# Values as the stationary operand in two attentions, and one block of instructions for the layers and what follows

## The reference

```
x = x + L0_xattn(layernorm(x))   # 4 layers, each: rmsnorm, causal self attention (16 heads of 8), bias
                                 #   rmsnorm, cross attention over the context rows a window allows
                                 #   rmsnorm, silu(gate) * up, down;   after the layers a last rmsnorm
x = x + L0_attn(layernorm(x))    # ternary attention: u, v factors, sigmoid of products, sums
x = x + L0_ffn(layernorm(x))
x = x + L1_xattn(context, layernorm(x))   # 2 heads of 64, 1601 context rows a batch
x = x + L1_attn(layernorm(x))    # causal self attention, 16 heads of 8
x = x + L1_ffn(layernorm(x))     # 8 experts of 512, the best two are summed

def sdpa(q, k, v, bias):
    s = einsum('bhqd,bhkd->bhqk', q, k) * scale + bias
    p = softmax(s)
    return einsum('bhqk,bhkd->bhqd', p, v)
```

## Time and profile before

| | us |
|---|---|
| median of 3 runs | 509.67 (509.57 to 510.04) |
| profiled execution, its own time | 507.16 |
| profiled execution, span | 505.0 |
| TensorE (PE) busy | 463.1, 92% |
| VectorE (DVE) busy | 360.1, 71% |
| ScalarE (ACT) busy | 267.4, 53% |
| GpSimd (POOL) busy | 227.3, 45% |

### The profile page before, as it was taken

How to read it: one execution, slowest core, us unless ns; L and a number is a source line. 1 busy time by engine, 2 the same in 40 slices (tenths; PEclk the granted TensorE clock), 3 DMA queues, 4 the chain that set the end, 5 groups by cost and what they waited for, 6 DMA issues and landing times. The chain is left out here.

```text
span 505.0 us, 14335 instructions
## 1 busy us (share of the span) xinstructions
PE 463.1 (92%) x5430; PEld 400.6 (79%) x5430; DVE 360.1 (71%) x1028; ACT 267.4 (53%) x714; POOL 227.3 (45%) x342
## 2 busy tenths in 40 slices
PE   0899999999999999939899898999999999899997
PEld 0777896788778876929898787888888988689997
DVE  4286668566856685547788778998899987584644
ACT  3367756775777577613334455655555564432221
POOL 1393149315821682133599431749889511220000
PEclk9899999999999999969999999999999999999999
DMA  7800120102019000012202431040220000000000
GB/s 221 298 3 2 38 70 17 32 11 83 3 42 388 11 3 2 1 51 94 69 3 70 137 126 65 2 132 1 67 68 1 2 2 1 1 2 1 12 0 12
DMA packets 10031, 27.07 MB, mean 54 GB/s; under 512 B 1425, under 2 KB 4838, under 8 KB 9702
## 3 DMA queue, kind: packets, MB, share of 16 engines
q1 hardware_dynamic: 9958, 26.09, 15.4%
HBM read 25.82 MB, written 0.26 MB: 52 GB/s over the span
## 5 line engine op out<-in xcount | busy, mean ns | idle before, releaser
L893 POOL TENSOR_TENSOR rstd<-ss,par 128x1 f32<-128x1 f32 x52 | 28.6, 551 | 103.0 <-ACT sq L729 103.0
L749 ACT ACTIVATE pr<-sd 128x512 f32<-128x512 f32 x56 | 34.6, 627 | 6.0 <-DVE sd L802 5.6
L1264 POOL TENSOR_TENSOR xh<-xh,rsx 128x512 f32<-128x512 f32 (+1 forms) x32 | 29.8, 930 | 4.6
L1781 POOL TENSOR_TENSOR rstd<-mv,par 128x1 f32<-128x1 f32 x21 | 5.3, 250 | 57.6 <-DVE mv L1616 48.0
L1260 POOL TENSOR_TENSOR xh<-cx,mvx 128x512 f32<-128x512 f32 (+1 forms) x32 | 30.8, 962 | 0.7
L733 ACT ACTIVATE h<-y,rstd 128x128 f32<-128x128 f32 x48 | 19.2, 400 | 9.8 <-POOL rstd L893 9.3
L1239 DVE BATCH_NORM_STATS2 stx<-cx 128x6 f32<-128x128 f32 x104 | 22.7, 275 | 0.7 <-DMA cx<-ctx_in 0.7
L887 POOL TENSOR_TENSOR kblk<-qk,cf 128x512 f32<-128x512 f32 x20 | 20.9, 1043 | 0.9
L879 POOL TENSOR_TENSOR qk<-rope 128x256 f32<-128x256 f32 x20 | 14.5, 726 | 13.7 <-DVE rope L786 13.6
L1249 POOL TENSOR_TENSOR rsx<-rsx,par 128x13 f32<-128x13 f32 x8 | 20.1, 2516 | 0.6
L729 ACT ACTIVATE sq<-y 128x129 f32<-128x129 f32 x52 | 15.9, 307 | 8.4 <-DVE y L833 6.7
(11 more groups left out here) (566 smaller groups left out, 1522.8 us busy)
## 6 DMA issues: line engine op xcount, KB each, us to landing
cx<-ctx_in SPq DMA_DIRECT2D x13, 768.0 KB
we<-we_in SPq DMA_DIRECT2D x8, 514.0 KB, 8.7
wc<-wc_in SPq DMA_DIRECT2D x4, 768.5 KB, 5.9
wa<-wa_in SPq DMA_DIRECT2D x5, 387.0 KB, 3.0
wb<-wb_in SPq DMA_DIRECT2D x4, 256.5 KB, 4.1
uvT<-uvT_in SPq DMA_DIRECT2D x1, 1024.0 KB, 4.8
uv<-uv_in SPq DMA_DIRECT2D x1, 1024.0 KB, 6.8
cx<-ctx_in SPq DMA_DIRECT2D x13, 32.5 KB
```

Of the source, the lines that this page charges most:

```text
L749: nc.scalar.activation(pr[:, t, at:at + 512], sd[:, t, at:at + 512], ACT.Exp).then_inc(s[piece], 1)
L893: nc.gpsimd.tensor_tensor(rstd[:, t:t + 1], ss[:, t:t + 1], par[:, 1:2], ALU.pow).then_inc(s[piece], 1)
L1264: nc.gpsimd.tensor_tensor(part, part, rsx[:, b, tiles].unsqueeze(2).to_broadcast(shape), ALU.mult).then_inc(xm["c_normed"], 1)
```

## The change

1. `weigha`, `weighb` and `cweigh` swap their operands: the values (32 columns) are stationary, the turned weights stream (64 columns), each result lands in 32 rows of PSUM, already turned. The sums come from four more matmuls for each of the three pieces, with a constant block of ones `ones8` stationary and 128 columns streaming.
2. `recip` and `crecip` take the reciprocal of 128 x 128 in place of 128 x 16; `o` and `co` write `oT` directly. `turn_o` and `oT` are gone; `cturn_o` and `coT` are left to `whole` alone.
3. The values' bias is added in `vblk` (layers) and no longer in `oT`; it is loaded with `bo`, in two DMAs where there was one. The rows of `Wo` are reordered on the host to fit.
4. The first block: one zeroing activation (2048 columns) for two (1152 each), no memsets of ones, one more load for `ones8`.
5. The second and third block are one. `opening` runs the layers, then each engine goes on with what follows, with no barrier between. The queues are joined: `JOIN` = 3547581.86 is added to the places of what follows, so on each engine all pieces of the layers stand ahead of all that follow. Banks are handed out over the joint queue. `z_moments`, `z_power` and `z_norm` of tile 3 now stand with those of the others.
6. All tables of places are new, of the layers and of what follows. `th` has two buffers, and `qh` is made in place; the context is reloaded behind `c_normed` where it was behind `c_center`.

Core of the diff:

```diff
-PERIOD, SKEW = 94.96, (0.0, 6.64, 13.36, 19.85)
+PERIOD, SKEW = 95.07, (0.0, 6.64, 13.28, 19.91)
...
-FINAL = {"PE": {}, "ACT": {"square_f": 233.37}, "DVE": {"norm_f": 235.66, "x_f": 248.65, "z_moments": 253.29, "z_norm": 346.43},
-         "POOL": {"pow_f": 468.90, "z_power": 528.02}}
+FINAL = {"PE": {}, "ACT": {"square_f": 2709.04}, "DVE": {"norm_f": 16.76, "x_f": 18.75, "z_moments": 23.76, "z_norm": 32.91},
+         "POOL": {"pow_f": 678.03, "z_power": 5874.90}}
...
+JOIN = 3547581.86
+class Joint:
+    def __init__(self):
+        self.queue = {e: sorted([(w, 0, l, t, p) for w, l, t, p in FAST.queue[e]] + [(JOIN + w, 1, i, g, p) for w, i, g, p in LAST.queue[e]])
+                      for e in AT}
+        self.first = {e: 1 + max(n for n, z in enumerate(q) if z[1] == 0) for e, q in self.queue.items()}
...
-        q2 = sb("q2", [P, T, 2, P])
-        vblk = sb("vblk", [P, T, 2, 8, 2, 9])
+        vblk = sb("vblk", [P, T, 2, 8 * 32])
+        ones8 = sb("ones8", [P, 80])
+        q2 = sd[:, :, 0:2 * P].rearrange("p t (g q) -> p t g q", g=2)
...
-                for j in range(4 * (half == "b"), 4 * (half == "b") + 4):
-                    for b in range(2):
-                        last = nc.tensor.matmul(bank[L * b:L * b + L, 18 * j:18 * j + 18], pts[:, t, P * j + L * b:P * j + L * b + L],
-                                                vblk[:, t, b, j, :, :], start=True, stop=True)
+                for b in range(2):
+                    for k in range(4):
+                        j = 4 * half + k
+                        at = 32 * j - 16 * half
+                        nc.tensor.matmul(bank[32 * k:32 * k + 32, L * b:L * b + L], vblk[:, t, b, at:at + 32],
+                                         pts[:, t, P * j + L * b:P * j + L * b + L], start=not half and b == 0, stop=True, skip_group_check=True)
+                for k in range(4):
+                    j = 4 * half + k
+                    last = nc.tensor.matmul(bank[32 * k:32 * k + 32, P:2 * P], ones8[:, 16 - 16 * half:48 - 16 * half], pts[:, t, P * j:P * j + P],
+                                            start=False, stop=True, skip_group_check=True)
...
-                        last = nc.tensor.matmul(bank[L * b:L * b + L, 36 * g:36 * g + 36], pts[:, t, P * g + L * b:P * g + L * b + L],
-                                                vcblk[:, 2 * t + b, g, :, :], start=True, stop=True)
+                        nc.tensor.matmul(bank[32 * g:32 * g + 32, L * b:L * b + L], vcblk[:, 2 * t + b, g, :],
+                                         pts[:, t, P * g + L * b:P * g + L * b + L], start=b == 0, stop=True, skip_group_check=True)
+                for g in range(4):
+                    last = nc.tensor.matmul(bank[32 * g:32 * g + 32, P:2 * P], ones8[:, 48:80], pts[:, t, P * g:P * g + P],
+                                            start=False, stop=True, skip_group_check=True)
...
             elif piece in ("recip", "crecip"):
-                nc.vector.reciprocal(rv[:, t, :], ops[:, :, 8]).then_inc(s[piece], 1)
+                nc.vector.reciprocal(qk[:, t, 0, :], held(od, k, l, t)[:, P:2 * P]).then_inc(s[piece], 1)
             elif piece in ("o", "co"):
-                nc.vector.tensor_tensor(o[:, t, :].rearrange("p (h d) -> p h d", d=HD), ops[:, :, 0:8],
-                                        rv[:, t, :].unsqueeze(2).to_broadcast([P, H, HD]), ALU.mult).then_inc(s[piece], 1)
+                nc.vector.tensor_tensor(oT[:, t, :], held(od, k, l, t)[:, 0:P], qk[:, t, 0, :], ALU.mult).then_inc(s[piece], 1)
...
-            elif piece == "oT":
-                act.wait_ge(s["turn_o"], n)
-                nc.scalar.activation(oT[:, t, :], held(od, "turn_o", l, t)[:, 0:P], ACT.Identity,
-                                     bias=A[:, A_BV:A_BV + 1]).then_inc(s["oT"], 1)
...
-            dve.wait_ge(s["zeroed"], 2)
-            for a in range(2):
-                nc.vector.memset(vblk[64 * a:64 * a + 64, :, :, :, a, 8:9], 1.0)
-            for a in range(4):
-                nc.vector.memset(vcblk[32 * a:32 * a + 32, :, :, a, 8:9], 1.0)
...
         with nc.Block() as block:
             @block.tensor
             def _(pe):
+                def whole():
...
+                either(pe, lambda: opening(pe, x_pe_piece, pe_piece, "PE"), whole)
                 x_queue(pe, x_pe_piece, pe_piece, "PE")
```

More of the change, by code:

```diff
@@ L108, in __init__ @@
     def __init__(self, engines, when):
-        self.queue = {e: sorted((when(p, l, t), l, t, p) for p, layers in pieces for l in layers for t in range(T)
-                                if p[:2] != "z_" or t < T - 1)
+        self.queue = {e: sorted((when(p, l, t), l, t, p) for p, layers in pieces for l in layers for t in range(T))
                       for e, pieces in engines.items()}
@@ L142 @@
 XAHEAD = 3
[L143 to L149, removed]
-YAT = {
[L151 to L181, removed]
@@ L564, in take @@
                 return x_take(pe, piece, t, 0)
-            for p, i, j in od.bank[piece, l, t][2]:
-                pe.wait_ge(s[p], one(i, j))
+            for kind, p, i, j in od.bank[piece, l, t][2]:
+                if kind:
+                    x_wait(pe, p, x_count(p, i, j))
+                else:
+                    pe.wait_ge(s[p], one(i, j))
             return held(od, piece, l, t)
@@ L1478, in x_act_piece @@
             elif piece == "un0":
+                if i < 2:
+                    act.wait_ge(s["y3" if i else "y2"], one(LAYERS - 1, T - 1))
                 x_wait(act, "v1", i - 1)
@@ L1834, in _, with whole @@
             def _(act):
+                def whole():
+                    general(act, act_piece, "ACT", act_any)
+                    ahead(act, x_act_piece, "ACT")
+                either(act, lambda: opening(act, x_act_piece, act_piece, "ACT"), whole)
                 x_queue(act, x_act_piece, act_piece, "ACT")
@@ L1838, in _, with whole @@
             def _(dve):
+                def whole():
+                    general(dve, dve_piece, "DVE", dve_any)
+                    ahead(dve, x_dve_piece, "DVE")
+                either(dve, lambda: opening(dve, x_dve_piece, dve_piece, "DVE"), whole)
                 x_queue(dve, x_dve_piece, dve_piece, "DVE")
@@ L1842, in _, with fast, whole @@
             def _(pool):
+                pool_bias(pool, 0)
+                def fast():
+                    zero_context(pool)
+                    opening(pool, x_pool_piece, pool_piece, "POOL")
+                def whole():
+                    pool_queue(pool, GENERAL)
+                    pool.wait_ge(s["y3"], one(LAYERS - 1, T - 1))
+                    zero_context(pool)
+                    ahead(pool, x_pool_piece, "POOL")
+                either(pool, fast, whole)
                 x_pool_start(pool)
```

321 lines of the change are left out of this document (197 added, 124 removed).

## The result

The changed kernel takes 502.16 us (median of four runs, 501.93 to 503.84) where the kernel before takes 509.83: ratio 0.9885, 95% interval 0.9859 to 0.9910. (That ratio and its interval are the record's; the two medians by themselves give 0.9850.) Predicted were 501.1 us and faster. In two later groups of runs the ratio was 0.9916 (0.9888 to 0.9944) and 0.9887 (0.9856 to 0.9919).

A forecast was written before the change was run, and what follows sets the result against it. TensorE was taken to bound the layers. Start -0.9, layers -2.8, boundary -4.5 and last part -0.4 sum to -8.6: 507.16 becomes 498.56, plus 2.51 gives 501.1 us; own range 497 to 505, for all 494.5 to 512.

The forecast's parts named there:

- offset of 2.51: Added to the sum because the profiled execution took 507.16 us and the median of the runs shown was 509.67.
- Start: First block: without DVE's memsets, TensorE's first matmul comes earlier, -0.9 us.
- TensorE in the layers: TensorE's queue: -1.4 us a layer, 0.98 from dropping turn_o and 0.4 from shorter weigh and cweigh, four strips at once.
- The reciprocal's duration: DVE in each attention: 128 columns take 0.97 us, +0.7; bounds 0.29 and 2.0.
- What of it is exposed: Layers: one of eight reciprocals a layer on the path, in self attention where DVE is near full, +0.7 us a layer.
- The new order: New places of everything else: 0, with 4 us allowed either way; as a rival, losing had chance 0.10, 505 to 510.
- The boundary: Between layers and what follows: barrier and waiting go, DVE's branch remains; along 4.5 us earlier, bounds 3.1 and 7.
- The last part: Four self attentions behind the layers: -0.5 for turn_o, -0.2 for eight halves, +0.3 for reciprocals, together -0.4 us.
- DVE taking over: Rival, chance 0.12: reciprocals exposed in the attentions, between shift and the next tile's max; slower from 17 exposed, 513 with 21.
- No low clock: Rival, chance 0.20: reciprocals covered and TensorE keeps the full clock level after its shorter pause; -14.2, 495.5 us.
- Two strips: Rival, chance 0.08: weigh and cweigh run two strips at once instead of four, 0.45 us more each, +25, 527 us.
- The first rival: Reciprocals covered and no low clock behind the layers, chance 0.20: -14.2, 495.5 us.

The follow-up runs named there:

- second profile: The changed kernel, unchanged, profiled once more; span 499.1 us, against 502.0 in its first profile.
- old places and copies: Changed kernel with its layers queued by the earlier kernel's places, and a plain copy replacing each attention reciprocal: 495.25 us, ratio 0.9786.
- order strip by strip: Changed kernel with the value matmuls of weigh and cweigh ordered so both key halves follow directly in one strip: 505.22 us.
- old places: Changed kernel with only its layers queued by the earlier kernel's places, period and skew: 499.9 us, ratio 0.9850; again 498.24 us, 0.9826.

## Why the prediction came out as it did

The sign was right and the total lies in the range, but its closeness is in part luck. The sum said -8.6. By medians the gain was 7.7 us in the first group of runs and 4.1 and 6.2 in the two later ones; by the ratios it was 4.3 to 5.9; by the spans it is 3.0 with the late dip and 5.9 in the second profile. Against that second profile the layers came out 6.3 us worse than forecast (+3.5 for -2.8), the boundary 1.1 better (counted to `M1`) and the rest 2.5 better, so that errors of both signs leave 2.7. The offset of 2.51 was taken from the group in which the kernel before was slowest (509.67, later medians 1.3 to 3.0 lower), and there 501.1 lies near 502.16.

- **Start**, -0.9: measured -0.7, and -0.9 in the second profile. Right.
- **TensorE in the layers**, -1.4 a layer: with old places and copies, where the two costs below are out of the way, the layer is 47.49 for 48.63, -1.14; some waits moved there too (`turna` and `turnb` +0.27, `cturn` -0.32). `turn_o` was charged 1.01, where 0.98 was counted. The gain of `weigh` was not there: 247 + 333 = 580 ns a half, where the earlier trace rows had 578 and 550 to 570 was forecast; `cweigh` gained 0.1 of the 0.16. The steps were read right, 56 and 109 ns for 59 and 112, and four strips do run at once; entry and exit took 138 ns and not 114 or less. The Trainium skill's figure for column tiles (TensorE: Matmul & The Clock Gate, Measured speedup vs the span model), which would have made 580 of the 460 ns beside an entry of 114, is not borne out: 466 is what is left. That the strip changes at every matmul was no reason for it, as the order strip by strip shows.
- **The reciprocal's duration**, 0.97 us by the slope of two rows: 0.954 to 0.957. The Trainium skill's repeat count (VectorE: DVE Perf Modes, First, the fixed hardware budget), with the clock from that page's Specifications, gave an estimate of 1.2, too long by a quarter.
- **What of it is exposed**, +0.7 a layer, in self attention: this is the first step that failed. It is 1.05 with old places and 1.64 with new ones, and 1.41 of the latter is in cross attention. The eight microseconds of the earlier trace rows show DVE full in self attention, and the prediction took the place where the engine is fullest for the place where a longer instruction counts. There TensorE has other tiles' work to do between `weigh` and `out`. In cross attention `cout` stands close behind `cturn` or `gate`, and what it waits for is `co`. No full DVE is in play there, since it stood idle before each `crecip`: the reciprocal's own length counts, in a chain of 2.15 us that TensorE has too little other work to cover. The new places take `up` out of that time in two tiles; the charge at `gate`, 4.31 for 3.92, holds 0.4 of the 0.6 that the two costs share.
- **The new order: 0, give or take 4.** The second step that failed, for it is zero in neither place: in the layers it costs 1.05 us each, 4.2 in all, and behind them up to 2.9 is gained where the late dip doesn't come. The bound of 4 held for the sum of the two, not for the layers. So layers are -1.14 + 1.05 + 1.05 = +0.96 each.
- **The boundary**, -4.5: measured -5.4 between the two traces; the barrier put back costs 6.1 at `M1` and 3.0 to 4.6 in the total. The mechanism was the stated one, down to the wait of `uT1` for DVE's branch. At `along` itself it is -3.8 (15.53 us behind the start of the last `down` before, 11.75 after), 0.7 less than forecast, because DVE needed 3.9 us from its branch to `uT1` where 3.1 was counted; and `M1` follows `along` 1.25 us later where it took 2.86.
- **The last part**, -0.4: part of the 2.9; the new order there was never undone by itself, so the two can't be told apart.
- **The rivals.** DVE taking over was half right, though not in the place that it named: the reciprocals cost 6.6 us in the layers, as much as nine exposed at 0.7, and it needed 17 of them. No low clock: it still came, for 6.8 us instead of 10.2. Two strips: no (its 527 is 526 by its own terms). The first rival's -14.2 wasn't reached even with old places and copies both, where the ratio of 0.9786 is -10.8.

What stays open: what the new places behind the layers are worth by themselves, what sets the length of TensorE's branch, and why the late dip of the clock comes in some executions.

## What to carry to other kernels

An operation that becomes longer costs where the consumer stands close behind in the bounding engine's queue, not where its own engine is fullest: measure the distance between producer and consumer in the bounding engine's queue for every place where the operation stands. When an edit changes durations and a new order comes with it, cross the two (old order with new work, new order with cheap work): each can carry a cost that the other hides, and here the old order with the new arithmetic is 4 us faster than the changed kernel. A sum that agrees with the total proves none of its terms.

## What the runs showed of the hardware that was not expected

- In column strips of 32, sixteen fp32 passes of 64 columns in four strips take 247 ns and the eight of 128 behind them 333; with four passes in a row in one strip, in place of two, it is 247 and 352.
- A branch over the other path took 3.71 us on TensorE in the changed kernel, and 4.82 with a copy for DVE's reciprocals as the only edit; on DVE 3.9 us pass from its branch to its next instruction.
- A pause in TensorE's work late in the kernel, 2.39 us busy of 3.50, was followed by 6.8 us at the low level in this trace; two of three profiles of the changed kernel have such a stretch there, and one of two of the version with old places, and it costs 2.0 us.
